# Token gathers of a mixture-of-experts stage: a bounds check instead of a clamped second index table

## The chip, the cores and the metric

The kernel runs on one core of a Trainium2 chip. The metric is the device time of one execution in microseconds (us). The engines that matter here are TensorE (PE), VectorE (DVE), ScalarE (ACT), GpSimd (POOL) and SyncE (SP); GpSimd issues the indirect transfers (gathers and scatters through a table of row numbers), SyncE most of the others.

## The reference

A decoder layer on 4 sequences of 512 tokens of width 512, in float32: windowed self-attention, cross-attention, and a mixture of experts, each on the layer-normed sum so far and added to it. Only the third part is touched by the change:

```
logits = xf @ router_weight;  topw, topi = top_k(softmax(logits), 8);  topw /= topw.sum()
CAP = 256                                   # slots of an expert, 64 experts, 2048 tokens
xe[e, pos] = xf[tok]                        # pos < CAP, else the token is dropped by this expert
h  = silu(xe @ gate[e]) * (xe @ up[e])      # 512 -> 192
ye = h @ down[e]                            # 192 -> 512
out[tok] += topw * ye[e, pos]
```

The 2048 x 8 picks are as many as the 64 x 256 slots, but they aren't spread evenly: some experts have more picks than slots, and others leave slots empty.

## The kernel before, in words

The kernel is four stages, one behind the other, each in a block of its own in which every engine has its own instruction stream and the engines meet through semaphores: self-attention, cross-attention (it also leaves the normed input of the experts in the DRAM tensor xn3, rows of 512 + 64 floats, and the router's logits), `route` (L1214) and `experts` (L1412).

`route` finds for each token its eight experts and its slot with each, and writes the softmax weights as the last 64 columns of xn3 (L1283, from SyncE, which waits until they are stored, L1284). Matmuls on one-hot matrices turn the slots about into a table by slot: `held[p, e, j]` is 1 + the number of the token in slot 128 j + p of expert e, or 0 where there is none. From it VectorE makes two integer tables (L1402 to L1408). `token` is held - 1, clamped at 0: an empty slot names token 0. `target` is held - 1 too, but an empty slot gets a number past the last token (2048 and up), through `spare` and `empty`.

`experts` goes through the 64 experts in order. Each has 256 slots as CT = 2 halves of 128 partitions. Rings of RING = 4 buffers hold the raw weights, the gathered rows `xg` (2 x 576 floats per partition and buffer) and the results `y`.

- GpSimd (L1491 to L1529) has its whole order written out, unrolled: a clear of a part of `hl`, gather(0), gather(1), and then for each e gather(e + 2) and add(e - 2). `gather(e)` (L1493) is two indirect transfers that read rows of xn3 by `token`; from e = 4 it first waits until both halves of y of expert e - 4 have been written (s_yA, s_yD), since these read the gates in xg. `add(e)` (L1503) waits for y of e, and for the adds of e - 2, and is two indirect transfers that add y to rows of the output (even e) or of `odd_sum` (odd e) by `target`, with a bounds check at 2047 that drops the rows of empty slots. At the end four direct transfers add odd_sum to the output (L1528).
- TensorE (L1653 to L1696) does, in step e: the gate and up products of e (L72 to L74), the eight transposes of xg of e + 1 (`turn`, L1659, behind the wait for the gathers, L1655), and the down product of e - 1. Before step 0 it does turn(0).
- ScalarE and VectorE split each float32 operand into a high part (L1543, L1548, L1549, L1554) and the rest (L1600, L1604, L1606, L1613), so that TensorE can multiply in three passes. They also compute silu and the product h, and y: half 0 on ScalarE (L1571), half 1 on VectorE (L1629), each scaled by the slot's gate from xg.
- SyncE (L1480 to L1489) loads the weights, four experts ahead.

Between two stages stand small blocks that clear the semaphores of the last stage and set those of the next one; no engine starts a stage before all have ended the one before.

Of the kernel before, what the change touches and what calls it, by code (L numbers as in the profile page):

```python
# [8 lines left out]
I32 = mybir.dt.int32  # L9
U32 = mybir.dt.uint32  # L10
ALU = mybir.AluOpType
# [3 lines left out]
P = 128  # L15
B, S, D = 4, 512, 512
T = S // P
NT = B * T
# [3 lines left out]
E, I, TOPK = 64, 192, 8  # L22
CAP = 256
CT = CAP // P
# [1186 lines left out]
        sp.dma_start(self.rawd[0:rest, i, 1, :], w[:, P:I, :].rearrange("a p d -> (a p) d")).then_inc(self.ld_d[i], 16)  # L1211

def route(nc, consts, logits, token, target, xn3, weights_of, odd_sum):  # L1214

# [2 lines left out]
    with ExitStack() as ctx:  # L1220
        m = Phase(nc, ctx, "ro")
# [17 lines left out]
        spare = m.sb("spare", [P, CT])  # L1239
        empty = m.sb("empty", [P, E, CT])  # L1240
        held = m.sb("held", [P, E, CT])
        tokenf = m.sb("tokenf", [P, E, CT])
        targetf = m.sb("targetf", [P, E, CT])
        column = m.sb("column", [P, NT, TOPK])
        row = m.sb("row", [P, NT, TOPK])
# [6 lines left out]
        zero = m.sb("zero", [P, D])  # L1252
        s_zero, st_zero = m.sem("zeroed"), m.sem("st_zero")
# [76 lines left out]
        def _(dve):  # L1330
# [56 lines left out]
            with dve.Fori(0, NT // 2) as r:  # L1387
                for i in range(2):
                    n = 2 * r + i
# [10 lines left out]
            dve.wait_ge(s_table, 1)  # L1400

            then(dve.tensor_copy(held[:].rearrange("p e j -> p (e j)"), table[:]))  # L1402
            dve.tensor_scalar(tokenf[:], held[:], -1.0, 0.0, ALU.add, ALU.max)
            then(dve.tensor_scalar(empty[:], held[:], 0.0, None, ALU.is_equal))
            then(dve.tensor_tensor(empty[:], empty[:], spare[:].unsqueeze(1).to_broadcast([P, E, CT]), ALU.mult))
            then(dve.scalar_tensor_tensor(targetf[:], held[:], -1.0, empty[:], ALU.add, ALU.add))
            dve.tensor_copy(token[:], tokenf[:].rearrange("p e j -> p (e j)")).then_inc(s_slot, 1)
            dve.tensor_copy(target[:], targetf[:].rearrange("p e j -> p (e j)")).then_inc(s_slot, 1)  # L1408
            dve.wait_ge(s_slot, 2)

def experts(nc, ident, token, target, xn3, weights_of, odd_sum, out):  # L1412

    R = I - P
    RING, DL = weights_of.AHEAD, 2
    PIECES = 4
    out_pieces, odd_pieces = [a.rearrange("(i n) d -> i n d", i=PIECES) for a in (out, odd_sum)]
    with ExitStack() as ctx:
        m = Phase(nc, ctx, "ex")
# [5 lines left out]
        xg = m.sb("xg", [P, RING, CT, XW])  # L1425
# [11 lines left out]

        ld_g = [m.sem(f"ld_g{k}") for k in range(RING)]
        st_y = [m.sem(f"st_y{k}") for k in range(RING)]
        st_out, s_zero = m.sem("st_out"), m.sem("zero")  # L1440
        counters = []

        def counter(name):
# [47 lines left out]
        @block.gpsimd  # L1491
        def _(pool):
            def gather(e):  # L1493
                if e >= RING:
                    pool.wait_ge(s_yA, START + e - RING + 1)
                    pool.wait_ge(s_yD, START + e - RING + 1)
                for j in range(CT):
                    at = CT * e + j
                    pool.indirect_dma_start(out=xg[:, e % RING, j, :], out_offset=None, in_=xn3,  # L1499
                                            in_offset=bass.IndirectOffsetOnAxis(token[:, at:at + 1], 0))\  # L1500
                        .then_inc(ld_g[e % RING], 16)

            def add(e):  # L1503
                pool.wait_ge(s_yA, START + e + 1)
                pool.wait_ge(s_yD, START + e + 1)
                if e > 1:
                    pool.wait_ge(st_y[(e - 2) % RING], 16 * CT * ((e - 2) // RING + 1))
                for j in range(CT):
                    at = CT * e + j
                    pool.indirect_dma_start(out=odd_sum if e % 2 else out, out_offset=bass.IndirectOffsetOnAxis(target[:, at:at + 1], 0),  # L1510
                                            in_=y[:, e % RING, j, :], in_offset=None, bounds_check=NT * P - 1,
                                            oob_is_err=False, compute_op=ALU.add)\
                        .then_inc(st_y[e % RING], 16)

            pool.memset(hl[R:2 * R, :, 1].bitcast(F32), 0.0).then_inc(s_zero, 1)
            gather(0)
            gather(1)
            for e in range(E):
                if e + 2 < E:
                    gather(e + 2)  # L1520
                if e >= 2:
                    add(e - 2)
            add(E - 2)
            add(E - 1)
            for k in range(RING):
                pool.wait_ge(st_y[k], 16 * CT * E // RING)
            for i in range(PIECES):
                pool.dma_start(out_pieces[i], odd_pieces[i], accum_op=ALU.add, max_dma_last_dim=8192).then_inc(st_out, 16)  # L1528
            pool.wait_ge(st_out, 16 * PIECES)  # L1529
# [169 lines left out]
def decoder_layer(nc, consts, x, context, w_qkv, w_out, b_out, wq, wk, wv, w_router, w_gate, w_up, w_down, out):  # L1699
# [4 lines left out]
    xn3 = nc.dram_tensor("xn3", (NT, P, XW), F32).ap()  # L1704
    rows = out.rearrange("b s d -> (b s) d")
    x2 = rows.rearrange("(n p) d -> n p d", p=P)
    with ExitStack() as ctx:
        ident, logits = [ctx.enter_context(nc.sbuf_tensor(*a)) for a in (("ident", [P, P], F32), ("logits", [P, NT, E], F32))]
        with nc.sbuf_tensor("stage", [P, 3 * C * D], F32) as stage, nc.semaphore("ld_wq") as ld_q, \
# [10 lines left out]
            with nc.Block() as block:  # L1720
                @block.sync
                def _(sp):
                    for s in w_w:
                        sp.sem_clear(s)
        token, target = [ctx.enter_context(nc.sbuf_tensor(*a)) for a in (
            ("token", [P, E * CT], I32), ("target", [P, E * CT], I32))]
        weights_of = ExpertWeights(nc, ctx, w_gate, w_up, w_down)
        odd_sum = nc.dram_tensor("odd_sum", (NT * P, D), F32).ap()
        route(nc, consts, logits, token, target, xn3, weights_of, odd_sum)
        experts(nc, ident, token, target, xn3.rearrange("n p d -> (n p) d"), weights_of, odd_sum, rows)  # L1730

# [47 lines left out]
```

## Time and profile before

| | |
|---|---|
| median of 3 runs | 1783.04 us (1779.92 to 1783.88) |
| the profiled execution | 1782.93 us, of which its span, first to last instruction, 1781.1 us |
| TensorE matmul, busy | 1478.7 us (83%) |
| VectorE, ScalarE, GpSimd busy | 1109.2, 1049.9, 610.0 us |
| gathers (L1499), 128 | 172.1 us, mean 1345 ns |
| scatters (L1510), 64 + 64 | 103.0 and 102.8 us, mean 1609 and 1606 ns |
| GpSimd's (software) DMA queue | 29248 packets, 72.53 MB |
| DMA of the whole kernel | 188.65 MB |
| mean granted TensorE clock | 0.919 of full speed |

Times in the views are us from the start of the span unless they are marked ns. A row of a timeline has start, duration, engine, line, operation, what it writes and reads, how many instructions, and in brackets how long the engine had been idle and what released it. The duration of an indirect transfer on GpSimd is the time in which GpSimd prepares it; the data move later, and "to landing" counts from its start to the data's arrival. "issue" as a releaser means that the profile shows nothing that the engine waited for. In the slices of the page a digit is a share in tenths, 40 slices over the span.

### The profile page before, as it was taken

How to read it: one execution, taken by the hardware profiler on the slowest of the kernel's cores; microseconds unless marked ns; L12 is line 12 of the kernel's file. 1: busy time of each engine (PE TensorE's matmuls, PEld its weight loads, DVE VectorE, ACT ScalarE, POOL GpSimd, SP SyncE). 2: the span in 40 equal slices, each digit the busy share in tenths (PEclk: the TensorE clock that was granted, in tenths of full speed). 3: DMA queues.
4: the chain of work that ended last, by engine and by line, in shares of the span. 5: the costliest groups of instructions: out<-in, count | busy, mean ns of one | idle time of the engine just before them, and what ended most of it. 6: DMA issues, size and time to landing. Idle time of an engine off the chain costs nothing. (4 is left out here: it accounts for less than half of the span.)

```text
span 1781.1 us, 30293 instructions
## 1 busy us (share of the span) xinstructions
PE 1478.7 (83%) x10066; PEld 1123.2 (63%) x10066; DVE 1109.2 (62%) x2035; ACT 1049.9 (59%) x2046; POOL 610.0 (34%) x436
## 2 busy tenths in 40 slices
PE   3988898988859798798887989435999999999990
PEld 2777676777747426525633842315899999999990
DVE  4667676667636426624813642577788888888880
ACT  3555455555534793694586479003677777777770
POOL 2444343444410000000000000021477777777772
PEclk9999999999979999999989989555899999999995
DMA  5000000000010002002002000421799999999986
GB/s 210 1 19 19 19 19 25 13 25 13 13 53 11 1 1 96 1 1 96 1 1 78 18 1 1 158 110 41 219 298 294 299 298 299 300 295 295 288 189 119
DMA packets 83620, 188.65 MB, mean 106 GB/s; under 512 B 13561, under 2 KB 13817, under 8 KB 83008
## 3 DMA queue, kind: packets, MB, share of 16 engines
q0 software_dynamic: 29248, 72.53, 18.3%
q1 hardware_dynamic: 53696, 113.74, 18.3%
q8 instruction: 71, 1.16, 0.3%
q10 hardware_dynamic: 576, 0.98, 0.2%
q14 instruction: 29, 0.24, 0.0%
HBM read 139.34 MB, written 55.05 MB: 109 GB/s over the span
## 5 line engine op out<-in xcount | busy, mean ns | idle before, releaser
L893 ACT ACTIVATE stage<-xa_ring 128x1024 f32<-128x1024 f32 x256 | 239.0, 1041 | 22.5 <-PE xa_ring L1115 22.5
L273 POOL TENSOR_TENSOR sa_prob<-sa_prob,sa_rinv 128x1024 f32<-128x1024 f32 x64 | 121.2, 1893 | 244.1 <-DVE sa_rinv L436 244.1
L793 POOL TENSOR_TENSOR xa_ve<-xa_mv,xa_eps 128x4 f32<-128x4 f32 x8 | 1.6, 200 | 581.0 <-DVE xa_mv L915 581.0
L1499 POOL DMA_INDIRECT ex_xg<-xn,token x128 | 172.1, 1345 | 82.9 <-issue 63.3
L331 ACT ACTIVATE sa_prob<-sa_sc_ps,sa_nmax 128x256 f32<-128x256 f32 x256 | 117.8, 473 | 110.9 <-DVE sa_nmax L423 110.9
L1127 PE MATMUL xa_out<-stage,xa_v 128*17 128x512 f32 x1024 | 139.7, 617 | 21.7 <-ACT stage L893 13.2
L72 PE MATMUL ex_ba<-ex_xh,ex_wh 128*128 128x256 f32 x512 | 150.6, 294 | 3.7 <-DVE ex_xl L1613 3.7
L74 PE MATMUL ex_ba<-ex_xh,ex_wl 128*128 128x256 f32 x512 | 145.8, 285 | 0.0
L73 PE MATMUL ex_ba<-ex_xl,ex_wh 128*128 128x256 f32 x512 | 145.7, 285 | 0.0
L1600 DVE TENSOR_TENSOR ex_wl<-ew_raw,ex_wh 128x1024 fp32r<-128x1024 f32 (+1 forms) x128 | 116.9, 955 | 35.9 <-ACT ex_wh L1543 35.9
L1031 DVE COPY xa_oT<-xa_out 128x512 f32<-128x512 f32 x32 | 22.1, 692 | 164.5 <-PE xa_out L1127 164.5
L423 DVE TENSOR_REDUCE sa_nmax<-sa_sc_ps 128x2 f32<-128x512 f32 x128 | 83.0, 687 | 65.7 <-PE sa_sc_ps L568 65.7
L1510 POOL DMA_INDIRECT out_dram<-ex_y,target x64 | 103.0, 1609 | 23.1 <-issue 23.1
L72 PEld LDWEIGHTS ex_ba<-ex_xh,ex_wh 128*128 128x128 f32 x512 | 98.6, 193 | 19.4 <-issue 19.4
L1510 POOL DMA_INDIRECT odd_sum<-ex_y,target x64 | 102.8, 1606 | 22.5 <-issue 18.9
L1543 ACT ACTIVATE ex_wh<-ew_raw 128x1024 fp32r<-128x1024 f32 (+1 forms) x128 | 100.2, 831 | 7.8 <-PEq L1450 7.8
L1104 PE MATMUL xa_ring<-ident,xa_stack 128*128 128x128 f32 x512 | 75.7, 290 | 32.8 <-DVE xa_stack L966 11.9
L1115 PE MATMUL xa_ring<-xa_qT,xa_kT 64*128 64x512 f32 x512 | 97.8, 461 | 5.6 <-DVE xa_qT L974 2.9
L1115 PEld LDWEIGHTS xa_ring<-xa_qT,xa_kT 64*128 64x128 f32 x512 | 40.2, 192 | 97.1 <-issue 92.7
L73 PEld LDWEIGHTS ex_ba<-ex_xl,ex_wh 128*128 128x128 f32 x512 | 99.0, 193 | 0.0
L74 PEld LDWEIGHTS ex_ba<-ex_xh,ex_wl 128*128 128x128 f32 x512 | 98.9, 193 | 0.0
L1104 PEld LDWEIGHTS xa_ring<-ident,xa_stack 128*128 128x128 f32 x512 | 61.4, 149 | 51.7 <-issue 25.2
(222 smaller groups left out, 4295.1 us busy)
## 6 DMA issues: line engine op xcount, KB each, us to landing
ew_raw<-in_L_ffn_gate_proj_dram SPq DMA_DIRECT2D x64, 384.0 KB, 5.7
ew_raw<-in_L_ffn_up_proj_dram SPq DMA_DIRECT2D x64, 384.0 KB, 7.6
ew_rawd<-in_L_ffn_down_proj_dram SPq DMA_DIRECT2D x64, 256.0 KB, 5.1
ew_rawd<-in_L_ffn_down_proj_dram SPq DMA_DIRECT2D x64, 128.0 KB, 6.5
sa_x<-in_x_dram SPq DMA_DIRECT2D x16, 256.0 KB, 2.7
x<-sa_x SPq DMA_DIRECT2D x16, 256.0 KB, 2.0
stage<-in_ctx_dram SPq DMA_DIRECT2D x16, 256.0 KB, 3.4
stage<-x SPq DMA_DIRECT2D x16, 256.0 KB, 4.4
```

The source lines that it names most:

```text
L72: pe.matmul(out, hi_l(c), hi_r(c), start=(c == 0), stop=False)
L73: pe.matmul(out, hi_l(c), lo_r(c), start=False, stop=False)
L74: last = pe.matmul(out, lo_l(c), hi_r(c), start=False, stop=(stop and c == chunks - 1))
L273: pool.tensor_tensor(prob[:, 4 * g:4 * g + 4, :], prob[:, 4 * g:4 * g + 4, :], rinv[:, 4 * g:4 * g + 4].unsqueeze(2).to_broadcast([P, 4, 2 ...
L331: act.activation(prob[:, h, :], sc_ps[p][:, i, :], ACT.Exp, bias=nmax[:, h:h + 1], accum_out=rsum[:, h:h + 1]).then_inc(s_ex[p], 1)
L893: act.activation(prob[:, u // 2 % 2, 2 * (u % 2):2 * (u % 2) + 2, :], ring[u % 3][:], ACT.Exp, scale=D2 ** -0.5).then_inc(s_ex[u % 3], 1)
L1104: last = pe.transpose(turn_banks[q % 2][:, a, :], stack[:, 2 * (4 * q + a):2 * (4 * q + a) + 2, :].bitcast(F32) .rearrange("p h w -> p (h ...
L1115: last = pe.matmul(ring[u % 3][:, i, :], kT[half, pair, kt * P:(kt + 1) * P], qT[half, pair, :], start=True, stop=True)
L1127: last = pe.matmul(out_ps[32 * i:32 * i + D2 + 1, :], v[:, kt, 4 * g + i, :], prob[:, w % 2, i, :], start=(kt == 0), stop=(kt == T - 1))
L1499: pool.indirect_dma_start(out=xg[:, e % RING, j, :], out_offset=None, in_=xn3, in_offset=bass.IndirectOffsetOnAxis(token[:, at:at + 1], 0))\
L1510: pool.indirect_dma_start(out=odd_sum if e % 2 else out, out_offset=bass.IndirectOffsetOnAxis(target[:, at:at + 1], 0), in_=y[:, e % RING, ...
L1600: dve.tensor_tensor(lo, src, hi.bitcast(F32), ALU.subtract).then_inc(s_wl, 1)
```

## The change

```diff
@@ route, L1402 to L1409
             then(dve.tensor_copy(held[:].rearrange("p e j -> p (e j)"), table[:]))
-            dve.tensor_scalar(tokenf[:], held[:], -1.0, 0.0, ALU.add, ALU.max)
             then(dve.tensor_scalar(empty[:], held[:], 0.0, None, ALU.is_equal))
...
-            dve.tensor_copy(token[:], tokenf[:].rearrange("p e j -> p (e j)")).then_inc(s_slot, 1)
             dve.tensor_copy(target[:], targetf[:].rearrange("p e j -> p (e j)")).then_inc(s_slot, 1)
-            dve.wait_ge(s_slot, 2)
+            dve.wait_ge(s_slot, 1)
@@ experts
-        st_out, s_zero = m.sem("st_out"), m.sem("zero")
+        st_out, s_zero, s_empty = m.sem("st_out"), m.sem("zero"), m.sem("empty")
@@ experts, gather(e)
                     pool.indirect_dma_start(out=xg[:, e % RING, j, :], out_offset=None, in_=xn3,
-                                            in_offset=bass.IndirectOffsetOnAxis(token[:, at:at + 1], 0))\
-                        .then_inc(ld_g[e % RING], 16)
+                                            in_offset=bass.IndirectOffsetOnAxis(target[:, at:at + 1], 0),
+                                            bounds_check=NT * P - 1, oob_is_err=False).then_inc(ld_g[e % RING], 16)
@@ experts, GpSimd's stream
             pool.memset(hl[R:2 * R, :, 1].bitcast(F32), 0.0).then_inc(s_zero, 1)
-            gather(0)
-            gather(1)
+            def empty(k):
+                pool.memset(xg[:, k], 0.0).then_inc(s_empty, 1)
+
+            pool.wait_ge(s_zero, 1)
+            for e in range(2):
+                empty(e)
+                pool.wait_ge(s_empty, e + 1)
+                gather(e)
             for e in range(E):
+                if e + 2 < RING:
+                    empty(e + 2)
+                    pool.wait_ge(s_empty, e + 3)
                 if e + 2 < E:
                     gather(e + 2)
```

The gathers read their rows by `target` and leave out the rows of empty slots, whose partitions of xg keep what stood there. So each of the four buffers of xg is cleared once, before its first gather. What the empty slots compute goes nowhere, as before, since the scatters drop it. The table `token`, its float form `tokenf` and the arguments that carry it are gone.

## Rows read from the trace of the kernel before

**Rows 1.** The page's 40 slices of the span: TensorE busy, and its granted clock

```profile
PE   3988898988859798798887989435999999999990
PEclk9999999999979999999989989555899999999995
```

**Rows 2.** Sums by stretch, experts' regular part: from:to, length, busy by engine, clock, DMA

```profile
1270.00:1724.50 454.50, 454.50 (x3247) 419.63 (x3246) 394.74 (x661) 356.22 (x722) 356.46 (x241) 1.00 1.04 290
```

**Rows 3.** Waits, 1271 to 1725, the longest: total us, times, longest us

```profile
ACT ex_sg L1558 <- PE ex_bb L74: 95.3, 60, 1.6
POOL ex_xg L1499 <- issue: 60.8, 119, 1.5
```

**Rows 4.** Chain of waits, 1500 to 1516: start, us, what; transposes of two experts

```profile
1506.78 0.87 PE ex_bx L1659 x8
...
1514.35 0.87 PE ex_bx L1659 x8
```

**Rows 5.** Timeline of GpSimd, one expert

```profile
1504.30 1.38 POOL L1499 DMA_INDIRECT ex_xg<-xn,token  x1 [0.70 <-issue]
1505.98 1.36 POOL L1499 DMA_INDIRECT ex_xg<-xn,token  x1 [0.30 <-issue]
1507.65 1.62 POOL L1510 DMA_INDIRECT odd_sum<-ex_y,target  x1 [0.30 <-issue]
1509.57 1.58 POOL L1510 DMA_INDIRECT odd_sum<-ex_y,target  x1 [0.30 <-issue]
1511.85 1.38 POOL L1499 DMA_INDIRECT ex_xg<-xn,token  x1 [0.70 <-issue]
...
DMA to landing us min/median/max: 6.3/7.0/7.6
```

**Rows 6.** Timeline of VectorE in the same expert: y, and the weights behind it

```profile
1502.73 0.73 DVE L1629 TENSOR_SCALAR ex_y<-ex_by,ex_xg 128x512 f32<-128x512 f32 x1
...
1505.26 1.83 DVE L1600 TENSOR_TENSOR ex_wl<-ew_raw,ex_wh 128x1024 fp32r<-128x1024 f32 x2 [0.48 <-ACT ex_wh L1543]
```

**Rows 7.** Timelines of GpSimd, VectorE and TensorE at the experts' start

```profile
1238.87 0.52 POOL L1515 MEMSET ex_hl<- 64x512 f32 x1 [56.97 <-POOLq L1450]
1239.75 1.24 POOL L1499 DMA_INDIRECT ex_xg<-xn,token  x1 [0.36 <-issue]
1241.29 1.28 POOL L1499 DMA_INDIRECT ex_xg<-xn,token  x1 [0.30 <-issue]
1242.87 0.95 POOL L1499 DMA_INDIRECT ex_xg<-xn,token  x1 [0.30 <-issue]
...
1240.50 1.83 DVE L1600 TENSOR_TENSOR ex_wl<-ew_raw,ex_wh 128x1024 fp32r<-128x1024 f32 x2 [5.44 <-ACT ex_wh L1543]
...
1246.51 1.94 PE L1659 MATMUL ex_bx<-ident,ex_xg 128*128 128x128 f32 x8 [13.23 <-DMA ex_xg<-xn,token]
```

**Rows 8.** Timeline of GpSimd at the experts' end: scatters, first direct accumulating transfer

```profile
1723.73 1.91 POOL L1510 DMA_INDIRECT out_dram<-ex_y,target  x1 [0.70 <-issue]
...
1740.41 1.56 POOL L1510 DMA_INDIRECT out_dram<-ex_y,target  x1 [0.30 <-issue]
1742.27 1.56 POOL L1510 DMA_INDIRECT odd_sum<-ex_y,target  x1 [0.30 <-issue]
...
1750.37 0.93 POOL L1528 DMA_DIRECT2D out_dram<-odd_sum  x1 [4.67 <-DMA odd_sum<-ex_y,target]
```

**Rows 9.** Timeline at the route's end (VectorE, SyncE's queue), and the gates' landing

```profile
1234.69 0.23 DVE L1407 CAST token<-ro_tokenf 128x128 int32<-128x128 f32 x1
1234.84 0.22 DVE L1408 CAST target<-ro_targetf 128x128 int32<-128x128 f32 x1
...
1232.67 0.38 SPq L1283 DMA_DIRECT2D xn<-ro_gates  x1
...
xn<-ro_gates SPq DMA_DIRECT2D x1, 512.0 KB, 3.3
```

**Rows 10.** Groups of GpSimd by line: clears of 2048 and 512 elements

```profile
L786 POOL MEMSET xa_stack<- 128x2048 f32 x1 | 1.8, 1807 | 0.0
L1289 POOL MEMSET ro_zero<- 128x512 f32 x1 | 0.5, 525 | 0.0
```

More of the change, by code:

```diff
@@ L1211, in load_down, with route @@
         sp.dma_start(self.rawd[0:rest, i, 1, :], w[:, P:I, :].rearrange("a p d -> (a p) d")).then_inc(self.ld_d[i], 16)
-def route(nc, consts, logits, token, target, xn3, weights_of, odd_sum):
+def route(nc, consts, logits, target, xn3, weights_of, odd_sum):
     NONE = E * CAP
@@ L1241, in route @@
         held = m.sb("held", [P, E, CT])
-        tokenf = m.sb("tokenf", [P, E, CT])
         targetf = m.sb("targetf", [P, E, CT])
@@ L1406, in _, with experts @@
             then(dve.scalar_tensor_tensor(targetf[:], held[:], -1.0, empty[:], ALU.add, ALU.add))
-            dve.tensor_copy(token[:], tokenf[:].rearrange("p e j -> p (e j)")).then_inc(s_slot, 1)
             dve.tensor_copy(target[:], targetf[:].rearrange("p e j -> p (e j)")).then_inc(s_slot, 1)
-            dve.wait_ge(s_slot, 2)
-def experts(nc, ident, token, target, xn3, weights_of, odd_sum, out):
+            dve.wait_ge(s_slot, 1)
+def experts(nc, ident, target, xn3, weights_of, odd_sum, out):
     R = I - P
@@ L1724, in _ @@
                         sp.sem_clear(s)
-        token, target = [ctx.enter_context(nc.sbuf_tensor(*a)) for a in (
-            ("token", [P, E * CT], I32), ("target", [P, E * CT], I32))]
+        target = ctx.enter_context(nc.sbuf_tensor("target", [P, E * CT], I32))
         weights_of = ExpertWeights(nc, ctx, w_gate, w_up, w_down)
         odd_sum = nc.dram_tensor("odd_sum", (NT * P, D), F32).ap()
-        route(nc, consts, logits, token, target, xn3, weights_of, odd_sum)
-        experts(nc, ident, token, target, xn3.rearrange("n p d -> (n p) d"), weights_of, odd_sum, rows)
+        route(nc, consts, logits, target, xn3, weights_of, odd_sum)
+        experts(nc, ident, target, xn3.rearrange("n p d -> (n p) d"), weights_of, odd_sum, rows)
 def constants():
```

## The prediction

> **What bounds the kernel now.** I read the 40 slices of the page first. TensorE is 9 or more in nearly every slice of the last third, and its granted clock is back at 9 tenths or more after the routing stage [rows 1]. The change lives in that last third, the expert stage. The sum over its regular part says what limits it: 454.5 us of span, 454.5 us with a matmul in flight, granted clock 1.00, at its level of 2.4 GHz; the DMA engines show a share of 1.04, VectorE 395 us, GpSimd 356 us [rows 2]. The waits of the same stretch have no TensorE row at all; the others wait for it, ScalarE 95.3 us over 60 experts [rows 3]. In the chain of waits, an expert's transposes come 7.57 us after the last one's [rows 4]. So an expert costs 7.57 us, and nothing that the change takes off another engine or the DMA queues can shorten that.
>
> GpSimd is the engine to look at next, because its 356 us leave out the time between its instructions. Over one expert [rows 5] it has gather 1.38, gather 1.36, scatter 1.62, scatter 1.58, with 0.30 us between them: 5.94 + 3 x 0.30. Then 0.70 us pass until the next gather. That gather waits for y of four experts ago; the VectorE instruction that writes it ends at 1502.73 + 0.73 = 1503.46, and the gather starts 0.84 us later [rows 6]. Where two scatters in a row wait for nothing, 0.30 is all that lies between them (1742.27 less 1740.41 + 1.56) [rows 8]. So GpSimd needs 5.94 + 4 x 0.30 = 7.14 us per expert of the 7.57 that it has: 0.43 us are free. That is the margin that decides this case.
>
> **The change part by part.**
>
> *Route.* Two VectorE operations go (the clamp and the cast of the token table). The cast starts 0.15 us before the next cast, and that one ends the stage's arithmetic at 1235.06 [rows 9]; the clamp costs the same in kind, so VectorE ends 0.3 us earlier. The stage's block ends only when SyncE has its gates stored as well: issued at 1232.67, 3.3 us to landing, 1235.97 [rows 9]. That is 0.9 us after VectorE, so the 0.3 us are covered: worth 0. Were the store gone, they would be worth 0.3 us.
>
> *Clearing the ring, first buffer.* Today GpSimd clears hl, then gathers at once [rows 7]. Now it clears hl, waits for that, clears 1152 elements per partition of xg, waits, and gathers. Clearing 512 elements takes 0.525 us and 2048 takes 1.807 [rows 10], so 0.835 ns per further element: 0.525 + 640 x 0.835 ns = 1.06 us. The two waits on its own semaphore are not in these rows: between 0 and, as the start after VectorE's y has it against the start without a wait (0.84 less 0.36 [rows 6, 7]), 0.5 us each. TensorE's first transpose starts at 1246.51, behind both gathers of expert 0 [rows 7], so all of this is on the path. Something comes back: the second gather takes 1.28 us beside VectorE's two weight operations of 1240.50 to 1242.33 and the third 0.95 without [rows 7]; moved by over 1 us, the second escapes them: up to 0.3. Bounds 0.8 and 2.1 us, I take 1.2.
>
> *The other three clears* (1.06 us each, before gathers 1 to 3) delay gathers that TensorE needs 7.6 us apart, while GpSimd then stands idle until the first y is stored. Expert 1's gathers slip by 2 to 3 us and are needed some 10 us after expert 0's: 0. Without that idle stretch each would cost its 1.06.
>
> *Fewer bytes.* A gathered row is 2304 bytes, a slot without a token costs one today, and about 9 in 100 slots are empty (by the reference's routing 1465 of 16384). That is about 3.4 MB less of the loads. It shortens landings, for which nobody waits (no TensorE row in [rows 3]): 0. If the landing ended last, it would be worth something; it doesn't.
>
> *The gather's own price*, 128 of them, is the unknown. A gather with a bounds check isn't in the trace. Below: nothing more than today's. It can't get cheaper, because GpSimd still walks all 128 indices, and the scatters, which drop the same slots, have 1.56 us at whatever expert in the quiet tail [rows 8]. Above: the scatter, which is indirect and checked but also accumulates. In quiet stretches the scatter takes 1.56 [rows 8], the gather 0.95 [rows 7]: 0.61 us apart. The direct accumulating transfer, with rows but no index and no check, takes 0.93 at its first [rows 8], about as much as the gather, so accumulating isn't free, and the 0.61 can't be given to the check alone or to the accumulation alone. I take half, 0.31 us a gather. The crowded slot makes it dearer: gathers stand just behind y, where VectorE is busy with weights [rows 6], and take 1.37 there against 0.95 (x1.44); a scatter placed there takes 1.91 against 1.56 [rows 5, 7, 8].
>
> Added as it is: 7.14 + 2 x 0.31 = 7.76 us, 0.19 over TensorE's 7.57. Stretched by 1.44: 7.14 + 2 x 0.45 = 8.04, 0.47 over. The longer gathers run partly into times when VectorE is off those operations, so I take 0.28. Gathers 4 to 63 stand in that regime: 60 x 0.28 = 17 us. At the full scatter's price in that slot (1.91 instead of 1.37) GpSimd needs 7.14 + 2 x 0.54 = 8.22, and 60 x 0.65 = 39 us are lost; with no price, nothing. On the start's path the same 0.31 counts twice: 0.6.
>
> **The rivals.** *The check is cheap (not slower).* If a checked gather costs under 0.43 / 2 = 0.21 us more in its slot, GpSimd stays inside 7.57 and TensorE keeps the bound; only the start is paid: 1783.04 + 1.2, with some of the check, 1784.5 us. For it: the gather's form is otherwise unchanged, and half of 0.61 is guesswork; against it: the margin is small and everything in the crowded slot is stretched.
>
> *The landing is late, GpSimd is not the bound.* The second gather is issued at 1505.98 and lands up to 7.6 us later, at 1513.6; TensorE takes up that expert at 1514.35 [rows 4, 5]. So 0.75 us are free there, in a ring that turns once in four experts. A gather longer by 0.2 pushes that landing by 0.4, and I would need one more late packet to break it: 0.3 us beyond the margin, over 4, times 60 is 4.5; 1789 us. Fewer bytes speak against it.
>
> *Relief pays (faster).* That needs TensorE to wait for data somewhere. It waits 13 us for the first gathers [rows 7] and not after; only the first landing, 5.2 us from the second gather's start to the first transpose, could shrink by the dropped rows, a tenth of it at most, 0.5 us. 1782.5 us at best.
>
> *The clock falls.* If TensorE idles 0.3 us in 7.6, it is as busy as in slices that read 8 and 9 now, and these show a clock of 9 [rows 1]. I add nothing.
>
> **How the numbers follow.** GpSimd becomes the bound: 0.47, 1802 us, its own range 1787 (a check just past the margin) to 1826 (1783 + 39 + up to 2.1 for the start and 1.1 for the price on its path, 1825 and a bit). Cheap check: 0.44, 1784.5. Late landing: 0.05, 1789. Relief: 0.04, 1782.5, and half of it could pass 0.2% only by a reading at the edge of the spread. This kernel's measurement can tell about 0.2%, 3.6 us, from no change: slower is 0.47 + 0.05 = 0.52, same 0.44, faster 0.04. The range reaches from the cheap check's low end, 1782, to the scatter's price, 1826, and 2 us of spread; beyond it I leave 1 in 10 or so.
>
> **What would show it.** Right: the gathers' group has a mean near 1.8 us; between a scatter and the next gather 0.30 us instead of 0.70; TensorE has waits for the landing of xg in the loop; its transposes come 7.8 to 7.9 us apart; bytes of the software queue down by 3.4 MB; the first transpose 1.2 to 2 us later against the clear of hl. Wrong: a gather mean under 1.55 and a gap that stays above 0.30, with the transposes still 7.57 us apart; then only the start's part stands. A first transpose at its old distance would put the clears beside something that I did not see. An expert time under 7.57 would mean that TensorE was not the bound.

## The result, and the profile after

The changed kernel takes 1790.67 us, the median of 5 runs (1787.20 to 1794.28), against 1783.04 for the kernel before (5 runs, 1779.92 to 1784.09). The ratio is 1.0046, with an interval from 1.0028 to 1.0064. In a second comparison, twelve runs of it gave 1790.46 against 1786.43 (35 runs): 1.0021, from 0.9999 to 1.0042. So it is slower, by 0.5% in the first comparison and by 0.2% in the second, whose interval just reaches no change; the traces below put the change's own part at 4.3 us, 0.24%. The forecast had the sign and held the time in its range, but was 11 us too high, and its large term stood for something that did not occur: the sign came from its small terms. The profiled execution took 1794.28 us (span 1792.5), 11.4 more span than before. That single pair exaggerates the change, as will be seen.

First the page's slices: TensorE's busy share and its granted clock, to set against [rows 1].

```profile
PE   3988888988859888898887989435899999999990
PEclk9999998999989999898989989555899999999995
```

The share of TensorE in the expert stage is what it was. The regular part of that stage, by sums (from:to, length, busy time by engine, granted clock, DMA share), answers to [rows 2]:

```profile
1280.00:1735.00 455.00, 453.69 (x3237) 418.38 (x3236) 396.65 (x660) 355.71 (x720) 358.72 (x240) 1.00 1.03 282
```

Before, TensorE had a matmul in flight in all of 454.5 us; now 1.31 us of 455 are empty. GpSimd's busy time has hardly moved (358.7 in 455.0 against 356.5 in 454.5). If it had become the bound, that number would have gone up by tens. The waits of this stretch, against [rows 3]:

```profile
ACT ex_sg L1564 <- PE ex_bb L74: 70.2, 45, 1.7
POOL ex_xg L1496 <- issue: 56.1, 117, 1.1
ACT ex_sg L1564 <- issue: 23.4, 15, 1.6
...
POOL ex_xg L1496 <- DVE ex_y L1635: 18.2, 3, 15.2
...
PE ex_ba L72 <- issue: 1.3, 2, 0.7
```

ScalarE's wait for TensorE is now told in two rows, 70.2 + 23.4 = 93.6 over 60 experts, so it still waits for TensorE. The last row is new: TensorE waits twice ahead of an expert's first gate product, for 1.3 us. That it names no landing ("issue") is taken up at the end. GpSimd in one expert, against [rows 5]:

```profile
1507.48 1.37 POOL L1496 DMA_INDIRECT ex_xg<-xn,target  x1 [0.77 <-issue]
1509.16 1.31 POOL L1496 DMA_INDIRECT ex_xg<-xn,target  x1 [0.31 <-issue]
1510.77 1.63 POOL L1507 DMA_INDIRECT out_dram<-ex_y,target  x1 [0.30 <-issue]
1512.71 1.82 POOL L1507 DMA_INDIRECT out_dram<-ex_y,target  x1 [0.30 <-issue]
1514.98 1.36 POOL L1496 DMA_INDIRECT ex_xg<-xn,target  x1 [0.45 <-issue]
```

The checked gathers take 1.37 and 1.31 us, as the unchecked ones did (1.38 and 1.36). GpSimd still stands idle for 0.45 to 0.77 us before it gathers. The chain of waits shows the distance of an expert's transposes from the last one's, first two experts as in [rows 4], then a stretch with one that is late:

```profile
1509.83 0.87 PE ex_bx L1665 x8
...
1517.40 0.87 PE ex_bx L1665 x8
```

```profile
1456.03 0.87 PE ex_bx L1665 x8
...
1463.59 0.87 PE ex_bx L1665 x8
...
1466.76 0.70 issue
...
1472.01 0.87 PE ex_bx L1665 x8
```

1517.40 less 1509.83 is 7.57, the old distance. 1472.01 less 1463.59 is 8.42: 0.85 us lost at one expert, and the 0.70 of "issue" between them is TensorE doing nothing. Call this a late expert. Measured by VectorE's first product of each expert, 58 of the 63 distances are 7.57. One at the start is 9.10 (7.62 before), and two pairs later are 7.72 and 8.26, 7.65 and 8.24. Before has none but its 7.62.

The experts' start, GpSimd and TensorE, against [rows 7]:

```profile
1246.10 0.52 POOL L1512 MEMSET ex_hl<- 64x512 f32 x1 [56.98 <-POOLq L1447]
1246.67 1.06 POOL L1514 MEMSET ex_xg<- 128x1152 f32 x1
1248.72 1.40 POOL L1496 DMA_INDIRECT ex_xg<-xn,target  x1 [0.99 <-POOL ex_xg L1514]
1250.43 1.02 POOL L1496 DMA_INDIRECT ex_xg<-xn,target  x1 [0.30 <-issue]
...
1253.33 1.01 POOL L1496 DMA_INDIRECT ex_xg<-xn,target  x1 [0.81 <-POOL ex_xg L1514]
```

```profile
1255.66 1.94 PE L1665 MATMUL ex_bx<-ident,ex_xg 128*128 128x128 f32 x8 [15.15 <-DMA ex_xg<-xn,target]
```

From the clear of hl to the first transpose it is now 1255.66 less 1246.10, 9.56 us; before it was 7.64. The quiet gather (1253.33) takes 1.01 us, 0.06 more than the 0.95 of before. At the end, a quiet scatter is still 1.56 [rows 8]:

```profile
1751.79 1.56 POOL L1507 DMA_INDIRECT out_dram<-ex_y,target  x1 [0.30 <-issue]
```

The bytes are down as worked out. The software queue of before and of after (packets, MB, share):

```profile
q0 software_dynamic: 29248, 72.53, 18.3%
```

```profile
q0 software_dynamic: 29248, 69.16, 17.8%
```

3.37 MB less in as many packets. A packet of the gathers holds two rows (4608 bytes, 8192 of them before); where both are dropped it stays behind with 8 bytes: the page counts 14285 packets under 512 bytes, 13561 before, 724 more. In 17 packets one row of the two is dropped, and 2 x 724 + 17 are the 1465 empty slots.

**Where the time lies.** I cut each trace at the same instructions: the clear of hl, the gather of expert 4, that of expert 63, the end of the span.

| us | before | after | before again | after again |
|---|---|---|---|---|
| self- and cross-attention (untouched) | 1142.0 | 1149.3 | 1146.2 | 1148.7 |
| route | 96.8 | 96.8 | 96.8 | 96.8 |
| clear of hl to the gather of expert 4 | 30.8 | 33.4 | 30.8 | 33.6 |
| gather of expert 4 to that of 63 | 446.5 | 448.2 | 446.5 | 448.1 |
| from there to the end of the span | 65.0 | 64.8 | 65.0 | 65.0 |

Only two rows move with the program: +2.6 at the start, +1.7 in the loop, 4.3 us in all. The untouched row differs by 7.3 us between the first two profiles and by 4.2 between two executions of the same kernel before. Over the fourteen profiles here (twelve kernels) it runs from about 1141 to 1151. The granted clock of these stages goes with it only roughly: its mean over the first 1140 us is 0.937 in before, 0.931 in after, and 0.931 in the second execution of before too. So 7 of the 11.4 us of the first comparison lie in stages that the change doesn't touch.

### The profile page after: what moved, and what is told of

Its sections match the earlier page's. It is cut to its first block and busy times, and to the rows that moved or that the text cites. A ratio compares the mean times of both kernels' runs of the same rounds, so it can differ in the third digit from the quotient of the medians.

```text
span 1792.5 us, 30424 instructions
## 1 busy us (share of the span) xinstructions
PE 1488.9 (83%) x10066; PEld 1131.5 (63%) x10066; DVE 1111.3 (62%) x2033; ACT 1051.3 (59%) x2046; POOL 618.3 (34%) x440
## 2 busy tenths in 40 slices
DMA packets 83621, 185.28 MB, mean 103 GB/s; under 512 B 14285, under 2 KB 14541, under 8 KB 83008
## 3 DMA queue, kind: packets, MB, share of 16 engines
q0 software_dynamic: 29248, 69.16, 17.8%
## 5 line engine op out<-in xcount | busy, mean ns | idle before, releaser
L1496 POOL DMA_INDIRECT ex_xg<-xn,target x128 | 170.8, 1335 | 79.0 <-issue 57.4
L1507 POOL DMA_INDIRECT out_dram<-ex_y,target x64 | 106.6, 1666 | 23.1 <-issue 23.1
```

## The experiments

**Both kernels again (e1, e2).** No edit. Two theories: what the first pair showed is the change's, or part of it is scatter.

> The kernel before, unchanged, timed against itself. Every theory expects a ratio of 1.000. Its use is the spread: if two sets of runs of one program can stand 3 to 5 us apart (the untouched self-attention and cross-attention stages of the profiled execution after ended 7.3 us later than those of before), this shows it. Its profile gives a second sample of the stages' lengths: route starts at 1142.0 us in before, at 1149.3 in after.

> The changed kernel, unchanged, timed again. Theory A (the clears at the experts' start are all that the change costs; the rest of the 7.6 us is scatter between executions of stages that are the same): +2.5 to +4 us, and the clear of hl to the experts' end 4 us longer than in before at most. Theory B (something in the changed program lengthens it everywhere, also in stages whose instructions are the same): +6 to +9 us again, with the route's start again some 7 us late. Theory C (GpSimd is near its limit and stumbles in the loop): the loop of gathers 4 to 63 is 2 us or more longer than 446.5.

Measured: e1 1786.91 against 1786.43, ratio 1.0000 (0.9980 to 1.0020). e2 1790.46, 1.0021 (0.9999 to 1.0042). The last two columns of the table are these traces. The late experts of e2 stand at the same places as in the first trace of after (distances of 7.74 and 8.22, 7.63 and 8.23), so they belong to the program and not to chance.

**The clears alone (e3).** The gathers are those of before.

```
+            def empty(k):
+                pool.memset(xg[:, k], 0.0).then_inc(s_empty, 1)
+
+            pool.wait_ge(s_zero, 1)
+            for e in range(2):
+                empty(e)
+                pool.wait_ge(s_empty, e + 1)
+                gather(e)
             for e in range(E):
+                if e + 2 < RING:
+                    empty(e + 2)
+                    pool.wait_ge(s_empty, e + 3)
...
```

> The kernel before with the four clears of xg and their waits alone; gathers by the clamped table, without a check. Theory A: +2.6 us (30.8 to 33.4 us between the clear of hl and the gather of expert 4), the whole cost of the change. Theory B: +2.6 and, if the longer program matters, up to the full +7.6. Theory C: +2.6, loop unchanged at 446.5.

Measured: 1787.26, ratio 1.0007 (0.9986 to 1.0028). The total can't tell, the trace can: clear of hl to first transpose 9.34, to expert 4's gather 33.26 (+2.4), second expert 9.09 us long, loop 446.48 as before, and no late expert. Nearly all of the start's cost is the clears'; none of the loop's is. GpSimd's rows differ from those of after in one point:

```profile
1246.58 1.06 POOL L1517 MEMSET ex_xg<- 128x1152 f32 x1
1247.95 2.02 POOL L1499 DMA_INDIRECT ex_xg<-xn,token  x1 [0.30 <-POOL ex_xg L1517]
```

Behind the same wait the first gather starts after 0.30 us instead of 0.99 and takes 2.02 instead of 1.40. So the 0.99 is not the price of the wait alone, and clear, gap and gather together are as long in both: 3.39 here, 3.45 in after.

**The check alone (e4).** Gathers by the old table, in which no index is out of bounds, so no row is dropped.

```
-                                            in_offset=bass.IndirectOffsetOnAxis(token[:, at:at + 1], 0))\
-                        .then_inc(ld_g[e % RING], 16)
+                                            in_offset=bass.IndirectOffsetOnAxis(token[:, at:at + 1], 0),
+                                            bounds_check=NT * P - 1, oob_is_err=False).then_inc(ld_g[e % RING], 16)
```

> The kernel before with a bounds check on the gathers, by the clamped table, so no row is dropped and nothing is cleared. Theory A: 0 to +0.3 us; quiet gathers 1.00 to 1.02 us instead of 0.95, crowded ones 1.3 to 1.4 as before. Theory C: +2 to +5, stumbles in the loop as in after. Theory B (a longer instruction stream, 128 register moves more): +3 to +5 and an early stage late again.

Measured: 1787.37, ratio 1.0005 (0.9984 to 1.0027). Quiet gather 1.00 (0.95 before), mean of the crowded ones 1.355 (1.366 before), start as before (30.87), loop 449.58: 3.1 more than before, with five late experts. GpSimd beside two of them, a scatter and the next gather:

```profile
1563.78 1.57 POOL L1510 DMA_INDIRECT out_dram<-ex_y,target  x1 [0.30 <-issue]
1566.77 1.08 POOL L1499 DMA_INDIRECT ex_xg<-xn,token  x1 [1.43 <-DVE ex_y L1629]
```

and the chain of waits over the same experts:

```profile
1560.91 0.87 PE ex_bx L1659 x8
...
1564.08 0.56 issue
...
1569.18 0.87 PE ex_bx L1659 x8
...
1572.35 0.80 issue
...
1577.69 0.87 PE ex_bx L1659 x8
```

8.27 and 8.51 us instead of 7.57. The gather's own price is 0.05 us quiet and nothing crowded, so the check is cheap, and GpSimd has idle time before its gathers (1.43 at 1566.77, where y itself is late). Behind y the checked gather starts after 0.91 us instead of 0.84. Still the loop is longer. The cost is not the gather's duration but a few experts that come late.

**The clears moved into the idle time of route (e5).** after, with xg allocated ahead and cleared whole, while GpSimd waits for the placement.

```
@@ route, GpSimd's stream
             pool.memset(zero[:], 0.0).then_inc(s_zero, 1)
+            pool.memset(xg[:].rearrange("p k j w -> p (k j w)"), 0.0).then_inc(s_clear, 1)
+            pool.wait_ge(s_clear, 1)
...
@@ experts, GpSimd's stream
             pool.memset(hl[R:2 * R, :, 1].bitcast(F32), 0.0).then_inc(s_zero, 1)
...
+            gather(0)
+            gather(1)
```

> The changed kernel with its four clears moved into the routing stage, where GpSimd waits 28 us for VectorE (xg is allocated ahead of that stage). Theory A (the clears cost the start 1.9 us and, by the clock that falls once more behind them, 0.6 us more): from the clear of hl to the gather of expert 4 back to 30.8 us from 33.4, the first expert-to-expert distance back to 7.62 us from 9.1, route's length unchanged at 96.8. Theory D (the check makes single gathers land too late for TensorE): the loop of gathers 4 to 63 stays 1.5 to 3 us above 446.5. Together +1.7 us against before; a rival (the clears also shift the loop's phase and cause its late experts) expects 446.5.

Measured: 1787.85 against 1785.25, ratio 1.0013 (0.9987 to 1.0040). From the clear of hl to expert 4's gather 30.84 us, as before, and the second expert takes its old 7.6. Loop 448.42, still 1.9 over before. So start and loop are two costs with separate causes. The start's rows in GpSimd's timeline:

```profile
1248.16 0.52 POOL L1513 MEMSET ex_hl<- 64x512 f32 x1 [57.08 <-POOLq L1448]
1249.11 1.30 POOL L1497 DMA_INDIRECT ex_xg<-xn,target  x1 [0.43 <-issue]
```

0.43 us between clear and gather here (0.36 in [rows 7]), against 0.05 + 1.06 + 0.99 in after. The clock shows where the rest of the start's 2.6 us came from. Sums by 2 us, with TensorE first and the granted clock third from the right, of after behind its first expert:

```profile
1266.10:1268.10 2.00, 0.09 (x1) 0.00 (x0) 1.94 (x4) 1.98 (x5) 0.00 (x0) 1.00 0.56 211
1268.10:1270.10 2.00, 1.72 (x13) 1.75 (x14) 1.97 (x5) 1.98 (x4) 0.00 (x0) 0.90 0.01 2
1270.10:1272.10 2.00, 2.00 (x11) 2.00 (x11) 1.43 (x3) 0.66 (x2) 0.00 (x0) 0.50 0.26 90
1272.10:1274.10 2.00, 2.00 (x15) 2.00 (x14) 0.52 (x1) 0.00 (x0) 0.00 (x0) 0.75 0.55 171
```

and of e5 in the same phase:

```profile
1268.00:1270.00 2.00, 0.65 (x5) 0.68 (x6) 2.00 (x5) 1.95 (x5) 0.00 (x0) 1.00 0.00 0
1270.00:1272.00 2.00, 2.00 (x19) 2.00 (x18) 1.39 (x3) 1.73 (x3) 0.00 (x0) 1.00 0.00 0
```

TensorE is empty for 2.2 us in both (1266.2 to 1268.4 in after, 1267.2 to 1269.4 in e5), but in after the clock is then granted at half (1.2 GHz) from 1270 on, where e5 and before keep 1.00 (2.4 GHz). That makes the second expert 9.10 us, 1.48 more. Against it, the first expert reached the full clock sooner after its start: its gate and up products, from their first to the transposes that follow, took 6.05 us, before 6.92. So 1.92 to the first transpose, + 1.48, - 0.87 = 2.53, which is the 2.6.

**A pause in front of the second gather (e6).** before, with a small clear there, to give the gather a later start without a check (and a wait for the clear of hl ahead of gather(0), which left the start as it was).

```
+                    if j == 1:
+                        pool.memset(pause[:, e:e + 1], 0.0)
```

> The kernel before, unchecked gathers by the clamped table, with a clear of one element per partition (0.1 us) ahead of the second gather of each expert, so that this gather starts some 0.2 to 0.5 us later. Theory D (the margin between the second gather's landing and TensorE's transposes, 0.3 us at its least in the trace of before, is what breaks): late experts in the loop, as many as in the checked kernels or more, loop 448 to 455 us. Theory E (a pure delay of the gather does not matter; the check itself or the longer instruction stream disturbs the engines): 446.5.

Measured: 1788.37, ratio 1.0013 (0.9989 to 1.0037); loop 447.59, +1.1, one late expert of 8.71. GpSimd's timeline shows that the edit did not do what it was for:

```profile
1501.81 0.12 POOL L1501 MEMSET ex_pause<- 128x1 f32 x1
1502.12 1.36 POOL L1502 DMA_INDIRECT ex_xg<-xn,token  x1 [0.19 <-issue]
```

0.12 and 0.19 fill the 0.30 that lies between two gathers anyway. The second gather starts 1.69 us after the first, 1.68 in before. So a kernel with neither check nor later second gather has a late expert too. What it shares with after is more instructions in GpSimd's stream.

**A longer stream by waits that are always met (e7).**

```
+                    pool.wait_ge(s_zero, 1)
```

> The kernel before with one wait more ahead of each gather, on a semaphore that has long had its value: 128 instructions more in GpSimd's stream, as many as the checked gathers' register moves, and no check. Theory E in its form 'longer stream' (GpSimd's instruction fetches come every 96 us instead of every 122, and disturb others): late experts in the loop, 448 to 450 us. Theory D: 446.5, unless the added wait delays the gathers.

Measured, one run: 1781.28 against 1785.25. Loop 446.46, no late expert. But the program has 30293 instructions, exactly those of before (the page's first line): such a wait is put into the gather itself and adds nothing to the stream. The experiment did not test its question.

**The first gather ahead of the clear of hl (e8).** before, with one line moved.

```
-            pool.memset(hl[R:2 * R, :, 1].bitcast(F32), 0.0).then_inc(s_zero, 1)
             gather(0)
+            pool.memset(hl[R:2 * R, :, 1].bitcast(F32), 0.0).then_inc(s_zero, 1)
             gather(1)
```

> The kernel before with GpSimd's clear of hl behind the two gathers of expert 0 instead of ahead of them. All theories: the first transpose comes up to 0.88 us earlier against the stage's start (0.52 of the clear and the 0.36 behind it); against the end of the routing stage, as the clear of hl is no longer the first. It prices the same path that the change's clears lengthen, from the other side. A rival: the clock's rise is tied to something else and the gain is given back over the first two experts.

Measured, one run: 1791.10, of which the untouched stages are 1150.7, the top of their scatter. From route's first instruction to expert 4's gather it is 127.14 us, 127.64 in before: 0.5 us gained. But half of it is not the edit's: ScalarE's first instruction of the experts stands 0.27 us nearer to route's first than in before. Against that instruction the first gather has hardly moved. Before, to set against its 1239.75 in [rows 7], and e8:

```profile
1238.89 1.57 ACT L1543 ACTIVATE ex_wh<-ew_raw 128x1024 fp32r<-128x1024 f32 x2 [7.84 <-PEq L1450]
```

```profile
1247.23 1.58 ACT L1543 ACTIVATE ex_wh<-ew_raw 128x1024 fp32r<-128x1024 f32 x2 [7.84 <-PEq L1450]
1248.05 1.24 POOL L1499 DMA_INDIRECT ex_xg<-xn,token  x1 [57.84 <-issue]
```

0.86 us with the clear ahead of the gather, 0.82 without: 0.04 gained where up to 0.88 was expected. The clear of hl and the 0.36 behind it cost the first gather next to nothing.

**A longer stream that is really longer (e9, e10).** before, with one instruction ahead of each gather (e9) or two (e10) that count up a semaphore for nobody.

```
+                    pool.sem_inc(s_fill, 1)
```

> The kernel before (no check, no clears) with one increment of an otherwise unused semaphore ahead of each gather: 128 instructions more in GpSimd's stream, which can't fold into their neighbours as the waits did. Theory E (a longer stream, by its fetches, makes late experts): one to five late experts, loop 447.5 to 449.6, GpSimd's fetch packets some 96 us apart. Theory D (the gathers' time against TensorE's need decides): 446.5, or late experts only so far as the gathers' starts move by 0.05 us or more.

> The same with two increments ahead of each gather, 256 instructions more. Theory E: more late experts than with 128, fetch packets some 80 us apart, loop 449 or more. Theory D: as with 128, by the shift of the gathers.

Measured, one run each: 1783.06 and 1783.64 against 1784.47. The page counts 30362 and 30490 instructions, 69 and 197 more than before and not 128 and 256: the waits for y, which stood by themselves, are put into the new instructions. Loops 448.10 and 447.73 (446.48 in before), with late experts of 8.60 and 8.06, and of 8.69; quiet gather 0.95. So without any check the loop's loss comes back, +1.6 and +1.3. Nearly three times as many added instructions cost no more. The totals can't show 1.5 us here; the loop can, since its length repeats to 0.1 in kernels with the old stream (446.46 to 446.48 in before, e1, e3, e7 and e8). A late expert of e9 on GpSimd:

```profile
1366.91 1.03 POOL L1500 DMA_INDIRECT ex_xg<-xn,token  x1 [1.05 <-issue]
```

The gather at 1366.91 stands 1.05 behind the scatter instead of 0.7, a third of a microsecond late. It is expert 17's, though, and the time is lost at expert 16, from 1369.8 on, when this gather's rows can't have arrived (from start to landing it takes 3.9 us at the least in before, 6.7 on the median). The two come together; the one is not the other's cause by way of the data.

**Gathers that wait for their own half of y, with the check (e11).** The check alone (e4), where each of the two gathers waits only for the y that was read from its own half: the first for ScalarE's, the second for VectorE's.

```
-                if e >= RING:
-                    pool.wait_ge(s_yA, START + e - RING + 1)
-                    pool.wait_ge(s_yD, START + e - RING + 1)
                 for j in range(CT):
                     at = CT * e + j
+                    if e >= RING:
+                        pool.wait_ge((s_yA, s_yD)[j], START + e - RING + 1)
```

> The check-only kernel (loop 449.6, five late expert distances) with one edit more: each of an expert's two gathers waits only for the half of y that reads the gates in its own half of xg, so the first gather no longer waits for VectorE's half, which ends 0.7 us after ScalarE's. Theory D (margin): the first gather starts up to 0.4 us after the last scatter instead of 0.8 and both land 0.3 to 0.4 us earlier; late experts gone or fewer, loop 446.5 to 447.5. Theory E: the stream is as long as before, so the late experts stay, 448 to 450.

Measured, one run: 1783.46 against 1784.47. Loop 446.85, no late expert at all: every distance but the first (7.62) is 7.57. TensorE is busy in all 450.00 us from 1275 to 1725. GpSimd and VectorE in one expert:

```profile
1502.88 1.58 POOL L1509 DMA_INDIRECT out_dram<-ex_y,target  x1 [0.30 <-issue]
1504.76 1.12 POOL L1498 DMA_INDIRECT ex_xg<-xn,token  x1 [0.30 <-issue]
1506.19 2.02 POOL L1498 DMA_INDIRECT ex_xg<-xn,token  x1 [0.31 <-issue]
```

```profile
1506.07 1.83 DVE L1599 TENSOR_TENSOR ex_wl<-ew_raw,ex_wh 128x1024 fp32r<-128x1024 f32 x2 [0.42 <-ACT ex_wh L1542]
```

The gather now follows the scatter at 0.30: it no longer waits for y. The second one starts 0.12 us into VectorE's weight operation (1506.07 to 1507.90) and takes 2.02 us, far more than any price of a check, and nothing comes late. GpSimd has room. Set against the transposes that read them, the two gathers start 0.44 and 0.65 us earlier than in e4 (medians of experts 8 to 59), but the second ends no earlier (6.78 us ahead of them, 6.77 in e4). Only its worst case is better: never under 6.77, where e4 falls to 6.13. One caution: the edit also shortens the stream by 60 instructions (30361 against 30421), since each wait is now put into its gather. GpSimd's stream is still as long as e9's (940 instructions in both, 872 in before), and e9 has late experts, so the length alone doesn't make them.

**after, repaired (e12).** after with e5's clears, e11's waits and e8's order: everything at once.

> The changed kernel with all three mends: clears in the routing stage, each gather waiting for its own half of y, and the clear of hl behind expert 0's first two gathers' first. Against before: routing to the gather of expert 4 0.2 to 0.5 us shorter, loop 446.5 (theory D) or 448.4 (theory E, as in the early-clears kernel): -0.5 or +1.5 us of some 1785, in both cases inside the interval, so the profile's stages decide.

Measured: 1785.97 (12 runs) against 1784.47 (17), ratio 1.0008 (0.9987 to 1.0030). No late expert, TensorE busy in 450.00 of 450.00 us. From route's first instruction to expert 4's gather 126.94 (127.64 in before), then 446.84 (446.48), then 34.93 to the direct transfers (34.21). The 0.7 at either end is the same: the gathers at which the trace is cut now start 0.7 us sooner (e11 alone has it too), and e8's order adds nothing, as the first transpose stands 104.65 us behind route's first instruction in e5 and in e12. The stages the change can reach are within 0.4 us of before. It does not beat it: a change that takes bytes from queues for which nobody waits has nothing to gain, even with its costs gone.

## Why the prediction was right or wrong

**What bounds the kernel: right.** TensorE, 7.57 us an expert, before, after and in each experiment.

**Route, worth 0: right.** The stage is 96.8 us in all of these. Its block still ends with SyncE's store of the gates:

```profile
1239.90 0.38 SPq L1282 DMA_DIRECT2D xn<-ro_gates  x1
```

**Fewer bytes, worth 0: right,** 3.37 MB of the forecast 3.4. One caution: with the check alone and no row dropped the loop lost 3.1 us (e4), with rows dropped 1.6 to 1.9 (after, e2, e5). Whether the shorter loads have to do with that, one trace of e4 can't tell.

**The clears of the first buffer: the size was off.** The clear was worked out as 1.06 us and took 1.06. Around it 0.05 and 0.63 (0.99 less 0.36) were lost, together inside the bound of twice 0.5, the second over its own 0.5; e3, whose gather follows the same wait after 0.30 and then takes 2.02, shows that this isn't the wait's price alone. The second gather did become shorter (1.02 for 1.28), yet the transposes came no sooner for it: 1.92 us instead of 1.2 + 0.6. The agreement of 1.92 with 1.8 is luck in part, since the 0.6 was a price of the check that is not there. Left out altogether was the clock: "I add nothing" was written of the loop, where it held, and not asked of the start, where it cost 0.6 net.

**The other three clears, worth 0: right.** e3, which has them all, keeps its loop of 446.48.

**The gather's own price: this step failed.** "I take half, 0.31 us a gather", and with the crowding 0.28 of each expert, 17 us. Measured: 0.05 quiet, nothing crowded. The whole difference between the gather and the scatter had been split between check and accumulation by no evidence at all, and 0.05 of the 0.61 is the check's. In the sum it was the only large term. The condition of my rival (a price under 0.21) was met, so GpSimd never became the bound.
**The rivals.** The cheap check had the mechanism and gave 1784.5. It lacked the clock (0.6), part of the start (0.7) and the loop's 1.7. The late landing, at a chance of 0.05, asked for 0.2 us more per gather and then for a landing that TensorE waits for in every turn of the ring. The push was much smaller: a gather starts 0.91 us after y instead of 0.84, and at a few places of the program 0.3 to 0.4 more. And the landing is not what came late. The margin that I read as 0.75 is 0.58 by that expert's own landing. Over experts 4 to 63 of before, from the second gather's landing to the transposes that read it, it is 1.3 us on the median and falls to 0.27 at expert 5 and to 0.33 and 0.32 at experts 54 and 55, and before loses nothing by it. Where no row is dropped, the two gathers of an expert are 128 packets of 4608 bytes, so the last one of a late expert can be found in the trace. It had ended 2.18 us before the first transpose in e9 (expert 16), 1.63 in e6 (30), 1.13 and 2.73 in e4 (41 and 53), 0.70 in e10 (55); the least in before is 0.77. In four of the five the data were there in good time. At expert 55 GpSimd starts its first gather 1.64 us after y in before already (1.71 in after), and before comes through that.

**The total.** 4.3 us are the change's (2.6 + 1.7), and the medians of the first comparison differ by 7.6. The rest, 3.3, is inside the interval within which before can be told from itself (e1: 0.2%, 3.6 us), and the second comparison gave 4.0.

**What stays open.** Shown: late experts occur in each kernel with more instructions in GpSimd's stream than before's (after, e2, e4, e5, e6, e9, e10), in none with before's length (before, e1, e7, e8) and not in e3, which adds a few at the start only; and they are absent where each gather waits for its own half of y only (e11, e12), though these streams are longer than before's too. Not shown: what in the stream makes an expert late. The queue of GpSimd's instruction loads has packets about every 122 us in the loop of before, every 93 to 113 in after, e4, e6, e9 and e12, which fits the lengths only roughly. Over after, e2, e4, e5, e6, e9 and e10 there are eleven places where an expert takes over 8 us behind one of 7.6. At six of them such a packet lies within 3 us of the late expert's transposes (expert 27 in after and e2, 53 in e4, 40 in e5, 30 in e6, 16 in e9), where under one would be expected by chance, and at five there is none (55 in after, e2, e5 and e10, 41 in e4). The kernel before, e11 and e12 have such packets too, and no late expert.

Nor does a trace say what TensorE stood still for. At each of the eleven the late expert's own transposes are recorded at the old distance, 7.56 or 7.57, behind the wait for both gathers. What comes late is the signal to ScalarE: in e9,

```profile
1369.15 0.39 ACT L1559 ACTIVATE ex_sg<-ex_ba 128x256 f32<-128x256 f32 x1 [1.66 <-PE ex_bb L74]
1370.59 1.34 ACT L1555 ACTIVATE ex_xh<-ex_bx 128x512 fp32r<-128x512 f32 x2 [0.79 <-PE ex_bx L1660]
```

its copy of the transposed tokens starts 1.7 us after the first transpose instead of 0.74, and the gate products, which need the copies, follow late. In e4's expert 53 already the silu is late, 0.97 us behind the first transpose instead of 0.20:

```profile
1654.31 0.38 ACT L1558 ACTIVATE ex_sg<-ex_ba 128x256 f32<-128x256 f32 x1 [2.34 <-PE ex_bb L74]
```

It waits for products that stand ahead of the wait for the gathers, so no landing can explain it; in e6's expert 30 it is 1.34. In after ScalarE's copy of the second half stood 0.89 us idle,

```profile
1466.04 0.60 ACT L1560 ACTIVATE ex_xh<-ex_bx 128x512 fp32r<-128x512 f32 x1 [0.89 <-DMA sw_raw<-in_L_attn_W_qkv_dram]
```

behind a load of the first stage, long since done, so the name is wrong. The cause of the loop's 1.7 us stays open, and so does why e11's order removes it.

## What to carry to other kernels

Before a resource is called the next bound, find the price of the new form by itself: a difference between two rows that differ in three ways (check, index, accumulation) can't be divided by taking half. A margin is its minimum over the loop and not its value in the expert one happens to open: read as 0.75 us, it was 0.27 at its least. And a thin margin is not yet a cause: before that is said, look whether the data of the late steps had arrived; in four of five they had. A loop of 446.5 us lost 1.3 and 1.6 us to nothing but more instructions on an engine that isn't the bound (e9, e10). And work put in front of the first load of a stage can be paid in full, with the clock's answer to it on top (the clears of xg, e3), or hardly at all (the clear of hl, e8); moved into an idle stretch of the stage before, it cost nothing at the start (e5).

## What the runs showed of the hardware

- A bounds check on an indirect gather of 128 rows costs GpSimd 0.05 us (0.95 to 1.00). Its start behind y moves by 0.07 us (0.84 to 0.91). The same gather is 1.37 on the mean beside VectorE's weight operations and 2.02 when it starts inside one (e11). The Trainium skill, SBUF — State Buffer, "Who interferes with whom", has a VectorE operation with two SBUF inputs contend with GpSimd's reads, but infers that it leaves descriptor generation alone; these rows show the gather's preparation twice as long under just such an operation.
- Rows dropped by the check leave the packet count as it is: 29248 in both kernels, 3.37 MB fewer; a gather packet carries two rows and keeps 8 bytes when both are dropped (724 of them).
- Between a clear, a wait for it and a checked gather lie 0.80 to 0.99 us in after; with unchecked gathers 0.27 and 0.30 in e3. At the stage's start the first gather begins 0.86 us after ScalarE's first instruction with a clear ahead of it and 0.82 without (before, e8).
- The granted clock went back to half from about 1270 on, after TensorE had stood idle for 2.2 us, from 1266.2 to 1268.4 (after; e3 and e2 show the same 0.50). The same idling behind the first expert, 2.2 us too, left it at 1.00 in before and e5. It cost 1.48 us at one expert.
- More instructions in GpSimd's stream, which nothing waits for, bring late experts: 69 more cost 1.6 us in the loop (e9), 197 more 1.3 (e10).
- Stages that no edit touched differ by up to 10 us between executions, so a difference of 0.2% needs the trace's stages and not the total.
